# A recurrent step on TensorE in another order: the update gate directly behind the reset gate, three x pieces in one run

## What is computed

```python
def step(H, xs):
    xz, xr, xh = xs
    Z = jax.nn.sigmoid(xz + H @ Whz.T + bhz)
    R = jax.nn.sigmoid(xr + H @ Whr.T + bhr)
    H_tilda = jnp.tanh(xh + R * H @ Whh.T + bhh)
    H_new = Z * H + (1.0 - Z) * H_tilda
    Y = H_new @ Whq.T + bhq
    return (H_new, Y)
# x + transpose(all Y); xz, xr, xh are X @ W + b for the three gates
```

## Time and profile before

| | before |
|---|---|
| median of 3 runs | 525.94 us (525.78 to 526.23) |
| the profiled execution, its own time | 528.27 us |
| span of the profiled execution | 526.5 us |
| mean granted clock of TensorE, share of full | 0.993 |
| TensorE busy, matmuls / weight loads | 97% / 94% of the span |
| ScalarE, VectorE busy | 63%, 60% |
| DMA, mean over the span | 53 GB/s |

### The profile page before, as it was taken

The page is one execution under the profiler, slowest core; times in us unless marked ns, Lnnn a source line. Parts: engine busy times, 40 slices in busy tenths (PEclk is TensorE's granted clock), DMA queues, the critical chain, the costliest instruction groups (busy, mean ns, idle before and its releaser), DMA issues.

```text
span 526.5 us, 96122 instructions
## 1 busy us (share of the span) xinstructions
PE 511.4 (97%) x44212; PEld 493.9 (94%) x44212; DVE 317.7 (60%) x1929; ACT 329.6 (63%) x1800; POOL 0.2 (0%) x4
## 2 busy tenths in 40 slices
PE   7499999999999999999999999999999999999997
PEld 7399999999999999999999999999999999999996
DVE  0246666666666666666666666666666666666664
ACT  2256666666666666666666666666666666666664
POOL 0000000000000000000000000000000000000000
PEclk9989999999999999999999999999999999999999
DMA  5011111111112111111111111111111111111111
GB/s 174 26 40 45 55 50 50 53 47 50 55 45 54 50 45 55 50 50 55 45 50 55 45 55 50 49 53 48 50 55 45 53 51 45 55 50 48 54 48 52
DMA packets 57881, 27.66 MB, mean 53 GB/s; under 512 B 6928, under 2 KB 56976, under 8 KB 57872
## 3 DMA queue, kind: packets, MB, share of 16 engines
q1 hardware_dynamic: 56736, 26.63, 18.0%
q10 hardware_dynamic: 1136, 0.89, 0.5%
HBM read 18.98 MB, written 8.52 MB: 52 GB/s over the span
## 4 chain that ended last, share of the span: by engine, by line
PE 97%; issue 2%; DMA 0%; DVE 0%; ACT 0%; SPq 0%; DVEq 0%; ACTq 0%
PE r_ps L241 34%; PE c_ps L241 28%; PE z_ps L241 23%; PE y_ps L241 11%; DMA xres_sb<-in_xr_dram 0%; DVE o_sb L209 0%; ACT c_ps L151 0%; SPq L126 0%; DVE u_sb L227 0%; ACT c_sb L186 0%; ACT r_ps L151 0%; ACT z_ps L151 0%; DVE ones_sb L197 0%; DVE h_sb L232 0%; SPq L127 0%
## 5 line engine op out<-in xcount | busy, mean ns | idle before, releaser
L241 PE MATMUL c_ps<-xt_sb,wx_sb 128*32 128x64 f32 x4128 | 173.5, 225 | 2.1 <-issue 2.1
L241 PE MATMUL z_ps<-xt_sb,wx_sb 128*32 128x64 f32 x4128 | 163.7, 221 | 2.2 <-issue 2.2
L176 ACT ACTIVATE r_sb<-r_ps 128x32 f32<-128x32 f32 x512 | 91.4, 198 | 109.1 <-PE r_ps L241 101.6
L222 DVE TENSOR_TENSOR rh_sb<-r_sb,h_sb 128x32 f32<-128x32 f32 x512 | 90.0, 192 | 85.1 <-ACT r_sb L176 81.0
L241 PE MATMUL z_ps<-h_sb,whz_sb 128*32 128x32 f32 x8192 | 124.5, 198 | 1.1 <-issue 1.1
L241 PE MATMUL c_ps<-rh_sb,whh_sb 128*32 128x32 f32 x8192 | 122.8, 198 | 0.0
L241 PE MATMUL y_ps<-whq_sb,h_sb 128*32 128x128 f32 x2064 | 113.6, 280 | 0.3 <-DVE h_sb L232 0.3
L241 PE MATMUL r_ps<-xt_sb,wx_sb 128*32 128x64 f32 x4128 | 107.8, 219 | 3.2 <-issue 1.9
L241 PEld LDWEIGHTS z_ps<-h_sb,whz_sb 128*32 128x32 f32 x8192 | 109.3, 111 | 1.3 <-issue 1.3
L227 DVE SCALAR_TENSOR_TENSOR u_sb<-z_sb,c_sb 128x32 f32<-128x32 f32 x512 | 75.3, 189 | 54.3 <-ACT c_sb L186 54.3
L241 PEld LDWEIGHTS z_ps<-xt_sb,wx_sb 128*32 128x32 f32 x4128 | 101.2, 111 | 2.3 <-issue 2.3
(11 more groups left out here) (27 smaller groups left out, 369.3 us busy)
## 6 DMA issues: line engine op xcount, KB each, us to landing
xt_sb<-in_xt_dram SPq DMA_DIRECT2D x130, 64.0 KB, 1.8
xres_sb<-in_xr_dram SPq DMA_DIRECT2D x130, 64.0 KB, 1.8
out_dram<-o_sb SPq DMA_DIRECT2D x130, 64.0 KB, 1.6
wx_sb<-in_wx_dram SPq DMA_DIRECT2D x2, 256.0 KB, 3.7
wx_sb<-in_wx_dram ACTq DMA_DIRECT2D x1, 256.0 KB, 4.3
whz_sb<-in_whz_dram SPq DMA_DIRECT2D x1, 256.0 KB, 4.6
whr_sb<-in_whr_dram ACTq DMA_DIRECT2D x1, 256.0 KB, 5.4
whq_sb<-in_whq_dram SPq DMA_DIRECT2D x1, 256.0 KB, 5.7
```

The source lines that it names most:

```text
L176: nc.scalar.activation(r_sb[:, o], r_ps[:, o, here], ACT.Sigmoid).then_inc(s_r[o], 1)
L222: nc.vector.tensor_tensor(rh_sb[:, k], r_sb[:, k], old[:, k], ALU.mult).then_inc(s_rh[k], 1)
L241: return nc.tensor.matmul(ps, weights, moving, start=start, stop=False, skip_group_check=True, **kw)
```

## The change

The update gate's four parts come directly behind the reset gate's, and both x pieces for the candidate come behind them, in one run with the x piece for the update gate that was there already. The wait for `s_h[1]` therefore stands directly behind the last part of the reset gate (for u > 0), and the wait for `s_seed_c` stands behind the update gate (for s = 0). On ScalarE, for s = 0, the sigmoid of the update gate is placed ahead of the seed of the reset bank. `y_step` only gives a name to lines that stood in the loop. Nothing is added or left out.

```diff
-                    if s == 0:
-                        seed(r_ps[:, :, W * (1 - p):W * (1 - p) + W], R).then_inc(s_seed_r, CS)
                     act.wait_ge(s_z_ps, t + 1)
                     nc.scalar.activation(z_sb[:], z_view(p)[:, :, B * s:B * s + B], ACT.Sigmoid).then_inc(s_z, 1)
+                    if s == 0:
+                        seed(r_ps[:, :, W * (1 - p):W * (1 - p) + W], R).then_inc(s_seed_r, CS)
...
-                    if s == 0:
-                        pe.wait_ge(s_seed_c, t + 1)
-                    x_piece(q, N, pieces[0])
                     if u > 0:
                         pe.wait_ge(s_h[1], t + 1)
                     for o in range(K):
                         for k in range(K):
                             z_mm = columns(...)
                     z_mm.then_inc(s_z_ps, 1)
-                    x_piece(q, N, pieces[1])
+                    if s == 0:
+                        pe.wait_ge(s_seed_c, t + 1)
+                    for piece in pieces:
+                        x_piece(q, N, piece)
...
-                    if s == 0:
-                        pe.wait_ge(s_seed_y, t + 1)
-                    y_mm = y_piece(q, s)
-                    if s == CS - 1:
-                        y_mm.then_inc(s_y_ps, 1)
+                    y_step(t, q, s)
```

More of the change, by code:

```diff
@@ L176, in _ @@
                         nc.scalar.activation(r_sb[:, o], r_ps[:, o, here], ACT.Sigmoid).then_inc(s_r[o], 1)
+                    act.wait_ge(s_z_ps, t + 1)
+                    nc.scalar.activation(z_sb[:], z_view(p)[:, :, B * s:B * s + B], ACT.Sigmoid).then_inc(s_z, 1)
                     if s == 0:
                         seed(r_ps[:, :, W * (1 - p):W * (1 - p) + W], R).then_inc(s_seed_r, CS)
-                    act.wait_ge(s_z_ps, t + 1)
-                    nc.scalar.activation(z_sb[:], z_view(p)[:, :, B * s:B * s + B], ACT.Sigmoid).then_inc(s_z, 1)
                     if s == CS - 1:
@@ L264, in y_piece, with y_step @@
                 return last
+            def y_step(t, q, s):
+                if s == 0:
+                    pe.wait_ge(s_seed_y, t + 1)
+                last = y_piece(q, s)
+                if s == CS - 1:
+                    last.then_inc(s_y_ps, 1)
             def r_part(u, k, o, moving):
```

## The result

The kernel after takes **531.53 us** in the median of four runs (530.97 to 532.56); the kernel before took 526.09 us beside it (525.78 to 527.45). The ratio of the runs is 1.0095, with an interval from 1.008 to 1.011 (that of the two medians is 1.0103): 5.4 us slower, where 3.5 us were forecast. The predicted 529.4 us is 2.1 us short, the range up to 531.9 us holds the result.

What follows compares the result with a forecast made beforehand. The prediction took TensorE, busy for 97% of the span, as the bound. Its terms, 0.05 + 0.005 = 0.055 us a pass, x 64 = 3.5 us, led to a median of 529.4 us, range 525.3 to 531.9.

Steps and rivals of the forecast that it cites:

- the cover is the same sum, 0.60 us, in another order: TensorE's work between last reset part and first candidate part: one piece, four parts, two pieces, 0.60 us, unchanged by reordering.
- The wait behind the reset gate: Wait for the state's second half, directly behind the last reset part: 0.025 us each in u = 1, 3, +0.05 a pass.
- two of the checks that the prediction named: In u = 1 the update gate's first load 0.13 behind the last reset part's; first reset sigmoid 0.42 behind its matmul, u > 0.
- The rule that stood beside the sum: Semaphore increments serialize at about 26 ns, so the projection's increment may delay u = 2's reset sigmoid; some 528 us in all.
- The wait for the candidate's seed: Moved from the reset gate to behind the update gate's last load in u = 0, 2: +0.005 us a pass.
- The earlier update gate: On TensorE the update gate finishes 0.115 us sooner, but nobody on the path gains: zero.
- ScalarE's order: In u = 0, 2 the reset bank's seed goes behind the update gate's sigmoid, hidden with nothing to spare: zero, 0.01 at most.
- The state's second half in time by 0.02: Its semaphore is there at 415.08, the first load behind the reset gate starts at 415.10: wait satisfied by 0.02 us.
- The last check: What would make the forecast wrong: the update gate's load was priced by an x piece's, though a wait's price might differ.
- Rival (a): No price: the load behind the reset gate loses 0.025 us but following x pieces take it up; 525.9 us, chance 0.16.
- Rival (c): More waits on the path: full 0.025 behind the update gate, or late seed or state; 532.3 to 534.3 us, chance 0.11.
- Profiling adds 2.3 us: The median of the runs lies 2.3 us below the profiled execution's own time, taken as what profiling adds.

## Why the prediction came out as it did

**The sign and the range were right, the reason for the number was wrong.** Its size, 3.5 us against 5.4, came from terms that are not there: the price was put on a wait that is free, and the loss lies in a sum that was taken as unchanged. So the sign and the range came out by luck.

*The step that failed* is "the cover is the same sum, 0.60 us, in another order". It adds a part at 0.065 us and an x piece at 0.115 whatever stands ahead of them. Directly behind the reset gate a part costs 0.08, since nothing longer stands between eight short ones in a row. The stretch was 630 ns and became 676, all of it in the update gate (267 to 318); 17 to 26 ns of the difference reach the end of each step, 93 ns a pass. The prediction's 0.26/4 was read from parts with an x piece on either side and used for parts that have none ahead; and its 0.115 for an x piece was too little for the one behind the reset gate (133 ns). For the same reason the update gate's sigmoid came 0.07 us sooner and not the 0.115 that the prediction moved it by.

*The wait behind the reset gate*, +0.05 a pass, measured nothing. The row of before was read rightly (a load with a wait 0.13 behind, a sigmoid at 0.42), but the cause was taken from what stood beside it. In the kernel after the loads of u = 1 are:

```profile
417.04 0.11 PEld L241 LDWEIGHTS r_ps<-h_sb,whr_sb 128*32 128x32 f32 x1
...
417.14 0.11 PEld L241 LDWEIGHTS z_ps<-h_sb,whz_sb 128*32 128x32 f32 x1
417.15 0.11 PEld L241 LDWEIGHTS r_ps<-h_sb,whr_sb 128*32 128x32 f32 x1
```

The update gate's first load carries the wait, stands 0.10 behind the first load of the reset part, not 0.13, and goes ahead of one of that part's own loads. The Trainium skill, same page, section "The mechanism", says that a weight load is pulled ahead of matmuls in flight where its rows don't conflict or where it goes to the background buffer; by that rule, the trace agrees, for a load with a satisfied wait too. So two of the checks that the prediction named fell in the trace itself: the 0.13, and "0.42 in all steps with u > 0" (0.398 in u = 1 and 3, 0.423 in u = 2, as before). In u = 2 the late sigmoid has stayed, and it belongs to the increment, as does the 0.13. The kernel with the increment moved still has the seed's wait behind the reset gate of u = 2, and there the load that carries it is taken ahead again (0.10):

```profile
414.55 0.11 PEld L241 LDWEIGHTS r_ps<-h_sb,whr_sb 128*32 128x32 f32 x1
...
414.65 0.11 PEld L241 LDWEIGHTS c_ps<-xt_sb,wx_sb 128*32 128x32 f32 x1
414.66 0.11 PEld L241 LDWEIGHTS r_ps<-h_sb,whr_sb 128*32 128x32 f32 x1
```

In the kernel with an increment in every step, u = 1 has no wait there and its load stands 0.13 behind all the same (415.52 - 415.39). The rule that stood beside the sum named this cause; taken by itself it would have led to 528 us, also short, since it says nothing of the run of short parts.

*The wait for the candidate's seed*, +0.005 a pass: no price; in the kernel after the x piece behind the update gate starts 183 ns behind the sigmoid in u = 2, with the wait, and in u = 1, without it. *The earlier update gate*, gain zero: held. *ScalarE's order*, zero "with nothing to spare": held, though the load that waits for the seed does come 0.03 later (below), and the experiment on it alone shows what is behind the margin, 11.6 us.

*The state's second half in time by 0.02*: held, since the load went out when the stream wanted it.

*The last check*, a wait "whose price depends on which instruction is behind it", missed too: what depends on the neighbours is the pace of the matmuls, not the price of a wait. Of the signs, the steps into u = 1 and u = 3 did come out at the 1.95 that was named, but not for that reason: the steps into u = 2 and u = 0, to which the sum gave nothing by this wait, grew by 25 and 17 ns as well, and the chain repeats every 7.91, not 7.87 to 7.88. *Rival (a)* had the right price for the wait, none, but not by a loss that x pieces take up: there is no loss. Its time was wrong, since it too left the cover as it was. *Rival (c)* gave 532.3 to 534.3 us by a dearer second wait or a late seed. Both of its signs are in the trace, the candidate's first load 0.06 behind the end of R*H's first half and, 416.22 - 415.32 = 0.90 behind the sigmoid of u = 0, this load of the reset gate's x piece:

```profile
416.22 0.30 PEld L241 LDWEIGHTS r_ps<-xt_sb,wx_sb 128*32 128x32 f32 x16
```

Neither means what the prediction took it for. The candidate comes late by the run of short parts. The seed's 0.03 (it is 0.87 in the steps without a seed) doesn't reach the path: with ScalarE's old order the load stands at 0.87 in every step, and the kernel takes as long.

*Profiling adds 2.3 us*: wrong, as shown above. It did no harm to the number, which is the median of before plus 3.5 us either way.

**What stays open.** Why TensorE loses 20 ns at these places, 16 records apart, isn't settled. It isn't the wait (u = 0 of the kernel after has none at that place), nor the position in the stream, nor the distance from the loop's start. That the loss needs short matmuls in an unbroken run is shown by one kernel (the x piece between the halves) and its counterpart; what in the chip sets the distance is not shown. Whether the reset gate's own two increments have a part in these places wasn't tested, nor why two waits on one load cost 22 ns.

## What to carry to other kernels

A list of the same matmuls in another order isn't the same sum: where TensorE's stream is the bound, keep a longer matmul between runs of short ones, and read a duration from rows with the same neighbours. Before a producer is moved by 0.1 us, look for the last consumer that has less room than that: here the seed of the reset bank, once behind the update gate's sigmoid, had none left and Z*H 0.06 us. A semaphore increment is best put where no other engine waits for the next one from the same engine: 0.16 us ahead of it cost 25 ns here, 0.36 us ahead nothing.

## What the runs showed of the hardware that was not expected

- Two parts of 32 moved columns take 123 ns directly behind an x piece and 159 ns in the update gate when it follows the reset gate's short parts without a break.
- A satisfied wait on a weight load was free, and the load was still taken ahead; two on one load cost 22 ns.
- An increment by the output projection delays the reset gate's by about 25 ns (steps of 1952 against 1927 ns), and not where the new state is waited for in between (2010 against 2008 ns).
- Eight more matmuls ahead of the loop cost 24 ns at the loop's edge in every pass, four more cost nothing there; a projection behind the edge starts 1.57 us behind the sigmoid instead of 1.18.
- One execution had a stretch at 0.70 of the clock between 20 and 30 us, another with nearly the same work in the 10 us ahead of it (5.17 and 5.15 us busy) none; outside the steady passes it was 2.7 us longer.
